# Graph layer with 4 nearest neighbours on one core: x times W2 at the opening of the score stage, scaled rows stored once in fp32

## The chip, the cores and the metric

One core of one Trainium2 chip runs the program. The metric is device time in microseconds (us); lower is better. All matrices are fp32; "fp32r" marks the rounded form that TensorE multiplies in one pass.

## The reference, cut to what matters

```
d  = 1/sqrt(rowsum(A));   y = d * (A @ (d * x))          # A: 8192 x 8192, x: 8192 x 128
z  = leaky_relu(y @ W1 + b1, 0.1)
S  = exp(-sqrt(max(|z_i - z_j|^2, 0) + 1e-10) / 2), all but the 4 largest of each row set to 0
A2 = S + A;  d2 = 1/sqrt(rowsum(A2))
out = d2 * (A2 @ (d2 * x)) @ W2 + b2
result = layernorm(x + out)
```

## The kernel before

Rows are cut into 64 tiles of 128, 16 blocks of 512 (four tiles each) and 8 groups of 1024. Three engines' programs and a DMA queue are written out by hand; every engine works its own list in order, and semaphores tie the lists together.

**First stages (to about 1045 us).** A is read, summed by rows and multiplied with d * x * W1, then read again in part, and z is made, kept as a rounded half `zh` and a rest `zl`.

**Score stage (1045 to 2240 us).** For each tile j of each group g, TensorE makes 8 pairs of 128x512 scores (`scores`, lines 881 to 889), ScalarE copies each pair out of PSUM (line 1171) and from the third tile on writes squares into PSUM ahead of some pairs (`seed`, line 1156), and VectorE searches the 8 largest of the whole row and their places (`find`, lines 1654 and 1657). There are two score buffers: the copies of tile j wait for the search of tile j-2 (line 1163), the search of tile j for all its copies. Between the second and the third tile TensorE rebuilds rows of squares (`squares_row`), and the third tile waits for their copies (`copy_squares`). From the seventh tile on, A @ xg of the previous group is woven in: SyncE loads pieces of A, ScalarE and GpSimd round them (lines 1141, 1323), GpSimd makes the rests (line 1328), TensorE multiplies (lines 925, 926, 936). Once per group GpSimd works out d2 (`near_sums`, `scale_of_rows`), scales the group's rows of x (`scale_xg`), and splits them into a rounded half `xgh` (`high_of_xg`) and a rest `xgl` (`low_of_xg`). SyncE then stores three things (lines 705 to 709): xg as plain rows to `xs_dram` for the gathers, and both halves to `xh_dram` and `xl_dram`; then it loads the next group's x.

**Tail (from about 2240 us).** 124 "quads" of A, 1 MB each, are loaded by SyncE through six slots (`load_t`). 92 are rounded by ScalarE (`round_t`, line 1220), their rests made by VectorE (`rest_t`, line 1701) and multiplied by TensorE with both halves of the scaled rows (`quad`, lines 995 to 1001); 32 are plain fp32 products (line 985). The halves come back from DRAM, two 512 KB loads for each of seven groups (`load_xs`). Each block is finished beside the quads, in the order `FIN` and at the quads `FIN_AT` (f counts blocks in that order): GpSimd gathers 4 neighbour rows for each row with 16 indirect DMAs a block (line 1485), ScalarE weighs them (`weigh`, line 1231), VectorE adds them (`neighbours`), TensorE adds the sum to the block by products with the identity (`gathered`, line 1012); ScalarE or VectorE brings it to SBUF (`heavy_y`, `light_y`), TensorE multiplies by W2 (`times_w2`, line 1021), VectorE adds x and b2 and takes the moments, ScalarE normalizes and stores. The blocks of `LIGHTS` (0 to 8) have most of their sum made in the score stage; they are kept in `acc`.

```
for u in range(len(tail)):
    quad(u)
    for f in range(B):
        if u == FIN_AT[f]:
            gathered(f)
        if u == FIN_AT[f] + 2:
            times_w2(f)
times_w2(B - 1)
```

Of the kernel before, what the change touches and what calls it, by code (L numbers as in the profile page):

```python
# [34 lines left out]
W1_EARLY = 3  # L35
STEP_2 = 3
# [10 lines left out]
FIN_AT = (22, 28, 34, 41, 48, 55, 62, 69, 76, 83, 90, 97, 103, 109, 115, 123)  # L47
OPEN_T, SUM_AFTER, ACC_AT = 6, 4, (9, 20, 40)
# [81 lines left out]
def build(nc, x, xt, at, W1, b1, W2, b2, consts, out, xs_dram, xh_dram, xl_dram, acc_dram, d_dram):  # L130
# [48 lines left out]
    with ctx:  # L179
# [88 lines left out]
        yz_odd = sb("yz_odd", [P, 2, BC], at=top_of["xgl_odd"])  # L268
        y = (tmp[:, 0:BC], yz_odd[:, 0])
# [21 lines left out]
        for name, where in (("raw_sq", top_of["sqn"]), ("raw_z", top_of["zl"] + 3 * SLOT * 4),  # L291
                            ("raw_ring", top_of["ring"] + 3 * SLOT * 4)):
            raw_t.append(sb(name, [P, TB, BC], at=where)[:, :, :])

# [61 lines left out]
        sq_turned = sem("sq_turned")  # L356
        z2_ok = sem("z2_ok")
# [30 lines left out]
        s_split = sem("s_split")  # L388
# [22 lines left out]
        u_ok = sem("u_ok")  # L411
        yf_light = sem("yf_light")
# [119 lines left out]
        n_light = [sum(b in LIGHTS for b in FIN[:f + 1]) for f in range(B)]  # L532
        n_heavy = [f + 1 - n_light[f] for f in range(B)]
# [16 lines left out]

        def wait_yf(eng, f):

            if FIN[f] in LIGHTS:
                eng.wait_ge(yf_light, n_light[f])
            else:
                eng.wait_ge(yf_heavy, n_heavy[f])
# [101 lines left out]
        def _(sp):  # L658
# [30 lines left out]
            sp.dma_start(xg, x[:, 0:GT]).then_inc(s_xn, 16)  # L689

            def group_loads(g, odd, first):
                xgh_g, xgl_g = halves_of(odd)
                for k in range(count(g)):
# [8 lines left out]
                    if k == RAW - 1 + (NP0 // 2 if first else 0):  # L702
# [3 lines left out]
                        dst = xh_dram[bass.ds(g, 1)].rearrange("o p t d -> p (o t) d")  # L706
                        sp.dma_start(dst, xgh_g[:, :, :].bitcast(F32)).then_inc(s_split, 16)
                        dst = xl_dram[bass.ds(g, 1)].rearrange("o p t d -> p (o t) d")
                        sp.dma_start(dst, xgl_g[:, :, :].bitcast(F32)).then_inc(s_split, 16)
                    if k == RAW + (NP0 // 2 if first else 0):  # L710
                        sp.wait_ge(s_xg, 16 * (g + 1))
                        sp.dma_start(xg, x[:, bass.ds((g + 1) * GT, GT)]).then_inc(s_xn, 16)
# [15 lines left out]
            def load_xs(g):  # L728
                low = g if g < G - 2 else G - 1
                sp.dma_start(xsh[:, g * GT:(g + 1) * GT].bitcast(F32), xh_dram[g]).then_inc(s_xs[g], 16)  # L730
                dst = (xsl if g < G - 2 else xsh)[:, low * GT:(low + 1) * GT].bitcast(F32)
                sp.dma_start(dst, xl_dram[g]).then_inc(s_xs[g], 16)

            sp.wait_ge(s_split, 32 * (G - 1))
# [31 lines left out]
        def _(pe):  # L766
# [125 lines left out]

            def squares_row(i):
# [12 lines left out]
            def piece(g, odd, k):  # L906
# [8 lines left out]
                if opens(g, k):  # L915
                    if not (is_first(g) and u < BANKS):
                        pe.wait_ge(flushed, units_before(g) + u - BANKS + 1)
                    if k == 0:
                        pe.wait_ge(xg_ok, chain_of(g, is_first(g)))
# [20 lines left out]
            def group_pe(g, odd):  # L940
                for j in range(GT):
                    for c in range(NE):
# [7 lines left out]
                        if is_first(g) and (j, c) == (0, NE // 2):  # L950
                            turn_squares(1)
                        if is_first(g) and (j, c) == (PLAIN_TILES - 1, NE - 1):
# [16 lines left out]
            def quad(u):  # L969
# [20 lines left out]
                pe.wait_ge(s_xs[h * TB // GT], 32)  # L990
# [14 lines left out]
            def gathered(f):  # L1005
                light = FIN[f] in LIGHTS
                bank = PS[:, 4 + f % 2] if light else PS[:, (FIN[f] - HB) % 2]
                if f >= 2:
                    wait_yf(pe, f - 2)
                pe.wait_ge(gs_ok, TB * (f + 1))  # L1010
                for j in range(TB):
                    i = pe.matmul(bank[:, j * P:(j + 1) * P], gs[f % 2][:, j], ident[:, :],
# [796 lines left out]
```

## Time and profile before

| | before |
|---|---|
| median of 3 runs | 2687.81 us (2685.91 to 2693.51) |
| profiled execution, its own time | 2688.38 us |
| profiled execution, span | 2686.4 us |
| busy share PE / DVE / ACT / POOL | 92 / 86 / 60 / 45% |
| mean granted TensorE clock | 0.982 |

PE is TensorE, DVE VectorE, ACT ScalarE, POOL GpSimd, SP SyncE. A busy TensorE is modelled: a matmul of 512 columns shows 0.39 us but the next starts 0.23 us later. An fp32 product shows as two records, a rounded one as one. Times of rows are counted from the span's start.

### The profile page before, as it was taken

Reading aid. Unit: us, or ns where it says so; the run is one execution under the profiler, and the core shown is the slowest. Engines: PE = TensorE matmul, PEld = TensorE weight load, DVE = VectorE, ACT = ScalarE, POOL = GpSimd, SP = SyncE. Lnnn points to the kernel's source line nnn. Section 1 sums busy time; section 2 is a strip of 40 time slices with the busy share of each in tenths; the row PEclk is TensorE's granted clock in tenths of the full one; section 3 lists DMA queues with packets and bytes.
Section 4 is the critical chain, followed back from the end, with each engine's and each line's share of the span. In section 5 each row is a group of like instructions: output and inputs, shape, how many; then the busy total and the mean of one; then the engine's idle time right before and its main releaser. Section 6 shows DMA issues by size and latency. Waiting matters only on the chain.

```text
span 2686.4 us, 28877 instructions
## 1 busy us (share of the span) xinstructions
PE 2463.0 (92%) x9309; PEld 1707.4 (64%) x9309; DVE 2313.1 (86%) x1366; ACT 1607.0 (60%) x1811; POOL 1198.3 (45%) x987
## 2 busy tenths in 40 slices
PE   0467999999999999899999999999999998899998
PEld 0233444444577776577778787877778775566765
DVE  7998889886788887999999999989999877587886
ACT  0000000000276766899999999989998885477775
POOL 0000000000000000067787878778787895777772
PEclk9879999999999999999999999999999998999999
DMA  9999999997599991035555555546555569999995
GB/s 389 421 394 407 398 421 420 421 403 293 197 413 360 363 349 55 0 114 177 150 167 150 166 152 154 161 133 183 143 175 146 177 181 351 397 401 394 392 379 215
DMA packets 150332, 722.74 MB, mean 269 GB/s; under 512 B 19424, under 2 KB 27296, under 8 KB 88992
## 3 DMA queue, kind: packets, MB, share of 16 engines
q1 hardware_dynamic: 124384, 670.43, 66.5%
q0 software_dynamic: 18800, 37.77, 5.8%
q10 hardware_dynamic: 6992, 12.62, 1.4%
q8 instruction: 79, 1.29, 0.2%
q14 instruction: 77, 0.63, 0.1%
HBM read 684.53 MB, written 36.21 MB: 268 GB/s over the span
## 4 chain that ended last, share of the span: by engine, by line
PE 56%; ACT 13%; issue 10%; DVE 9%; DMA 8%; POOL 3%; SPq 0%; ACTq 0%; POOLq 0%; DVEq 0%
PE PS L779 19%; ACT R L1171 5%; PE PS L881 4%; PE PS L883 4%; PE PS L882 4%; DMA ring<-at 3%; PE PS L985 3%; PE PS L849 3%; PE PS L925 2%; PE PS L936 2%; PE PS L926 2%; DVE R L1654 2%; ACT PS L1156 2%; PE PS L845 2%; PE PS L846 2%
## 5 line engine op out<-in xcount | busy, mean ns | idle before, releaser
L1328 POOL TENSOR_TENSOR al<-ring,ah 128x1024 fp32r<-128x1024 f32 x264 | 643.6, 2439 | 179.7 <-ACT ah L1141 168.1
L1654 DVE MAX8 R<-R 128x8 f32<-128x8192 f32 x64 | 555.8, 8685 | 59.4 <-ACT R L1171 59.2
L1171 ACT ACTIVATE R<-PS 128x1024 f32<-128x1024 f32 x512 | 518.0, 1018 | 116.1 <-PE PS L889 85.9
L1657 DVE FIND_INDEX8 R<-R,R 128x8 uint32<-128x8192 f32 x64 | 555.8, 8685 | 0.0
L1301 POOL CAST zst<-zh 128x128 fp32r<-128x128 f32 (+1 forms) x64 | 26.3, 411 | 1112.7 <-DVE zl L1577 811.6
L881 PE MATMUL PS<-zh,zst 128*128 128x512 f32 x1024 | 407.8, 398 | 29.0 <-ACT PS L1156 12.1
L883 PE MATMUL PS<-zh,zst 128*128 128x512 f32 x1024 | 400.3, 391 | 0.0
L882 PE MATMUL PS<-zl,zst 128*128 128x512 f32 x1024 | 399.7, 390 | 0.0
L1485 POOL DMA_INDIRECT R<-xs_dram,R x256 | 283.8, 1109 | 86.1 <-issue 77.1
L1156 ACT ACTIVATE PS<-R 128x1024 f32<-128x1024 f32 x310 | 318.0, 1026 | 6.6
L779 PE MATMUL PS<-cache,R 128*128 128x512 f32 x584 | 259.6, 596 | 5.4 <-DVE R L1528 5.4
L1510 DVE TENSOR_TENSOR R<-R,cache 128x2048 f32<-128x2048 f32 x106 | 242.9, 2292 | 17.5 <-DMA cache<-at 15.0
L881 PEld LDWEIGHTS PS<-zh,zst 128*128 128x128 f32 x1024 | 192.4, 188 | 96.3 <-ACT PS L1156 24.9
L883 PEld LDWEIGHTS PS<-zh,zst 128*128 128x128 f32 x1024 | 192.5, 188 | 41.6
L882 PEld LDWEIGHTS PS<-zl,zst 128*128 128x128 f32 x1024 | 192.7, 188 | 38.9 <-issue 0.7
L779 PEld LDWEIGHTS PS<-cache,R 128*128 128x128 f32 x584 | 110.7, 191 | 140.2 <-issue 140.2
L779 PE MATMUL PS<-ring,R 128*128 128x512 f32 x384 | 176.4, 606 | 9.9 <-DVE R L1528 5.4
L1585 DVE TENSOR_TENSOR al<-ring,ah 128x2048 fp32r<-128x2048 f32 x66 | 151.0, 2290 | 30.7 <-ACT ah L1053 30.2
L1510 DVE TENSOR_TENSOR R<-R,ring 128x2048 f32<-128x2048 f32 x72 | 165.0, 2291 | 12.3 <-DMA ring<-at 10.4
L995 PE MATMUL PS<-ah_t,xsh 128*128 128x512 f32 x368 | 155.4, 422 | 18.6 <-ACT ah_t L1220 18.4
L1060 ACT ACTIVATE R<-PS 128x512 f32<-128x512 f32 x16 | 9.6, 597 | 255.8 <-PE PS L788 255.8
L1141 ACT ACTIVATE ah<-ring 128x1024 fp32r<-128x1024 f32 x152 | 159.7, 1051 | 3.3 <-DMA ring<-at 2.6
(190 smaller groups left out, 4376.4 us busy)
## 6 DMA issues: line engine op xcount, KB each, us to landing
R<-at SPq DMA_DIRECT2D x152, 1024.0 KB, 11.0
ring<-at SPq DMA_DIRECT2D x148, 1024.0 KB, 9.6
ring<-at SPq DMA_DIRECT2D x264, 512.0 KB, 3.9
cache<-at SPq DMA_DIRECT2D x117, 1024.0 KB, 17.1
raw_sq<-at SPq DMA_DIRECT2D x21, 1024.0 KB, 9.8
raw_z<-at SPq DMA_DIRECT2D x20, 1024.0 KB, 10.1
raw_ring<-at SPq DMA_DIRECT2D x20, 1024.0 KB, 8.6
acc_dram<-R POOLq DMA_DIRECT2D x78, 256.0 KB, 5.7
```

The costliest lines, as they stand in the source:

```text
L779: i = pe.matmul(PS[:, b % YB], xs[:, q * TB + k], slots_a[slot_of[n]][:, k], start=first and k == 0, stop=prod_at[b, q] == closed[b] and k ...
L881: pe.matmul(bank, zst[:, par, 0], zh[:, cols], start=not on_seed, stop=False, skip_group_check=True)
L882: pe.matmul(bank, zst[:, par, 0], zl[:, cols], start=False, stop=False, skip_group_check=True)
L883: i = pe.matmul(bank, zst[:, par, 1], zh[:, cols], start=False, stop=on_seed, skip_group_check=True)
L1141: act.activation(ah[:, k % SPLIT], raw[k % RAW], ACT.Copy).then_inc(rounded, 1)
L1156: act.activation(pair(False, 0, c), sq_row[c], ACT.Copy).then_inc(seeded, 1)
L1171: act.activation(score[j % 2][:, c * EC:(c + 1) * EC].rearrange("p (b c) -> p b c", b=2), pair(first, j, c), ACT.Copy).then_inc(copied, 1)
L1328: pool.tensor_tensor(al[:, k % SPLIT], raw[k % RAW], ah[:, k % SPLIT].bitcast(F32), ALU.subtract)\
L1485: pool.indirect_dma_start(gx[f % 2][:, j, m], None, xs_dram, bass.IndirectOffsetOnAxis(ap=sidx[:, FIN[f] * TB + j, m:m + 1], axis=0))\
L1510: v.tensor_tensor(total.rearrange("p (k c) -> p k c", c=BC), other, slots_a[slot_of[n]], ALU.add)\
L1654: v.max(top[:, j], score[j % 2]).then_inc(dve3, 1)
L1657: v.max_index(place[:, j], top[:, j], score[j % 2]).then_inc(placed, 1)
```

## The change

x is multiplied by W2 before anything else is done with it in the second half, so that A2 @ (d2 * x) comes out already multiplied. Eight products of eight tiles each are put into the first group's second to fifth tile; their result goes through PSUM banks 4 and 5 and `xw_out` to `xw_dram`, from which the groups are loaded in place of x. In the tail the product with W2 becomes a transposition; the gathered rows, now multiplied by W2 too and weighed by S * d2, are added by VectorE to x and b2, so `gathered` and `light_y` go. Of the scaled rows one more fp32 copy is stored (`xp_dram`) in place of two halves; in the tail it is loaded once per group, ScalarE rounds it (`high_of_xs`) and GpSimd subtracts (`low_of_xs`). The waits on `s_split` go; SyncE waits for `s_xp` ahead of the next group's load.

```diff
+W2_AT = [(j, c) for j in range(1, 5) for c in (2, 6)]
+LOW_AFTER = {4: (0, 0), 5: (0, 3), 6: (1, 2)}
# SyncE, ahead of the first group
-            sp.dma_start(xg, x[:, 0:GT]).then_inc(s_xn, 16)
+            sp.wait_ge(zl_ok, B)
+            for k in range(G):
+                if k >= 1:
+                    sp.wait_ge(w2_made, k)
+                sp.dma_start(xt_in[:, :, :], xt[:, k * GT:(k + 1) * GT]).then_inc(s_xt, 16)
+                if k >= 1:
+                    sp.wait_ge(w2_copied, k)
+                    sp.dma_start(xw_dram[:, (k - 1) * GT:k * GT], xw_out[:, :, :]).then_inc(s_xw, 16)
+                if k == 2:
+                    sp.wait_ge(s_xw, 16)
+                    sp.dma_start(xg, xw_dram[:, 0:GT]).then_inc(s_xn, 16)
...
# SyncE, each group
-                        sp.dma_start(dst, xgh_g[:, :, :].bitcast(F32)).then_inc(s_split, 16)
-                        dst = xl_dram[bass.ds(g, 1)].rearrange("o p t d -> p (o t) d")
-                        sp.dma_start(dst, xgl_g[:, :, :].bitcast(F32)).then_inc(s_split, 16)
+                        sp.dma_start(dst, xg).then_inc(s_xp, 16)
...
+                        sp.wait_ge(s_xp, 16 * (g + 1))
# SyncE, tail
-                sp.dma_start(xsh[:, g * GT:(g + 1) * GT].bitcast(F32), xh_dram[g]).then_inc(s_xs[g], 16)
...
-                sp.dma_start(dst, xl_dram[g]).then_inc(s_xs[g], 16)
+                sp.dma_start(low_tiles(g).bitcast(F32), xp_dram[g]).then_inc(s_xs[g], 16)
# TensorE
+            def x_w2(k):
+                pe.wait_ge(s_xt, 16 * (k + 1))
...
+                    pe.wait_ge(w2_copied, k)
+                for j in range(GT):
+                    i = pe.matmul(PS[:, 4 + j // TB, j % TB * P:(j % TB + 1) * P], xt_in[:, j], w2[:, :],
+                                  start=True, stop=True)
+                i.then_inc(w2_made, 1)
...
-                pe.wait_ge(s_xs[h * TB // GT], 32)
+                pe.wait_ge(xs_low, h * TB // GT + 1)
...
-                    i = pe.matmul(PS[:, 6 + f % 2, j * P:(j + 1) * P], yf[f % 2][:, j * P:(j + 1) * P], w2[:, :],
-                                  start=True, stop=True)
+                    i = pe.transpose(PS[:, 6 + f % 2, j * P:(j + 1) * P], rows[:, j * P:(j + 1) * P], ident[:, :])
...
-                    if u == FIN_AT[f]:
-                        gathered(f)
# ScalarE
+            def copy_x_w2(k):
+                act.wait_ge(w2_made, k + 1)
+                if k >= 1:
+                    act.wait_ge(s_xw, 16 * k)
+                act.activation(xw_out[:, :, :].rearrange("p (h j) d -> p h (j d)", h=2), PS[:, 4:6], ACT.Copy)\
+                   .then_inc(w2_copied, 1)
...
+                        if first and (j, c - 1) in W2_AT:
+                            copy_x_w2(W2_AT.index((j, c - 1)))
...
+            def high_of_xs(g):
+                act.wait_ge(s_xs[g], 16)
+                act.activation(xsh[:, g * GT:(g + 1) * GT], low_tiles(g).bitcast(F32), ACT.Copy).then_inc(xs_high, 1)
...
+                    if u == tail.index((HB, g * GT // TB)) - 1:
+                        high_of_xs(g)
# GpSimd
-                pool.tensor_copy(sval[:, tiles], near[:, lo:hi])
+                pool.tensor_tensor(sval[:, tiles_of(g, early_part)], near[:, lo:hi], bcast(tiny[:, 4, lo:hi], KNN),
+                                   ALU.mult).then_inc(sval_ok, 1)
...
+            def low_of_xs(g):
+                pool.wait_ge(xs_high, g + 1)
+                pool.tensor_tensor(low_tiles(g), low_tiles(g).bitcast(F32), xsh[:, g * GT:(g + 1) * GT].bitcast(F32),
+                                   ALU.subtract).then_inc(xs_low, 1)
# low_of_xs(0 to 3) stand ahead of the gathers, the other three after gathers (f, j) of LOW_AFTER
# VectorE
-            def light_y(f):
...
+                v.wait_ge(gs_ok, TB * (f + 1))
+                lt(v.tensor_tensor(xb[f % 2], xb[f % 2], gs[f % 2], ALU.add))
```

## Rows read from the trace of the kernel before

**Rows 1.** The page: the span.

```profile
span 2686.4 us, 28877 instructions
```

**Rows 2.** Stretches: length; busy us of PE, PEld, DVE, ACT, POOL; clock, DMA share, GB/s.

```profile
1045.00:1190.00 145.00, 124.75 (x502) 92.38 (x501) 137.97 (x26) 122.62 (x130) 36.49 (x49) 0.99 0.11 35
2240.00:2330.00 90.00, 75.83 (x233) 46.33 (x234) 52.59 (x54) 37.35 (x48) 53.13 (x45) 0.91 1.02 401
2330.00:2640.00 310.00, 299.74 (x1250) 215.04 (x1248) 254.43 (x480) 222.83 (x357) 241.36 (x216) 1.00 1.01 391
```

**Rows 3.** Timeline of VectorE, opening: start us, us, instruction, [idle before it].

```profile
1065.12 8.68 DVE L1654 MAX8 R<-R 128x8 f32<-128x8192 f32 x1
...
1086.07 8.70 DVE L1654 MAX8 R<-R 128x8 f32<-128x8192 f32 x1 [3.36 <-ACT R L1171]
```

**Rows 4.** Timeline of ScalarE, opening of the score stage.

```profile
1060.83 1.02 ACT L1171 ACTIVATE R<-PS 128x1024 f32<-128x1024 f32 x1 [0.78 <-PE PS L889]
...
1084.00 1.92 ACT L1171 ACTIVATE R<-PS 128x1024 f32<-128x1024 f32 x2
...
1103.71 1.03 ACT L1171 ACTIVATE R<-PS 128x1024 f32<-128x1024 f32 x1 [2.44 <-DVE R L1657]
```

**Rows 5.** Groups by line, whole run: busy us, mean ns | idle before, releasers.

```profile
L1328 POOL TENSOR_TENSOR al<-ring,ah 128x1024 fp32r<-128x1024 f32 x264 | 643.6, 2439 | 179.7 <-ACT ah L1141 168.1 <-PE PS L936 1.2 <-POOL d2s L1383 1.0
L1485 POOL DMA_INDIRECT R<-xs_dram,R x256 | 283.8, 1109 | 86.1 <-issue 77.1 <-DMA xs_dram<-R 8.4 <-DVE R L1715 0.6
L1141 ACT ACTIVATE ah<-ring 128x1024 fp32r<-128x1024 f32 x152 | 159.7, 1051 | 3.3 <-DMA ring<-at 2.6 <-PE PS L926 0.5
...
L1012 PE MATMUL PS<-ident,R 128*128 128x128 f32 x128 | 16.8, 274 | 0.0
...
L1727 DVE TENSOR_TENSOR R<-R,b2r 128x512 f32<-128x512 f32 x16 | 10.9, 682 | 0.0
...
L1722 DVE TENSOR_TENSOR R<-PS,R 128x512 f32<-128x512 f32 x9 | 6.2, 688 | 8.7 <-PE PS L1012 8.6
...
L814 PE MATMUL PS<-ident,dsc 128*64 128x128 f32 x1 | 0.3, 273 | 0.0
```

**Rows 6.** Waits, 2330 to 2640 us: us in total, times, longest.

```profile
ACT ah_t L1220 <- PE PS L1001: 30.1, 20, 4.6
...
ACT ah_t L1220 <- DMA raw_z<-at: 9.2, 3, 3.4
```

**Rows 7.** DMA issues, whole run: KB each, median us from issue to landing.

```profile
R<-xs_dram,R POOLq DMA_INDIRECT x256, 5.9
...
xs_dram<-R SPq DMA_DIRECT2D x7, 512.0 KB, 3.5
xsh<-xh_dram SPq DMA_DIRECT2D x7, 512.0 KB, 14.3
```

**Rows 8.** Timeline of GpSimd, gathers of the tail.

```profile
2275.32 1.06 POOL L1485 DMA_INDIRECT R<-xs_dram,R  x1 [8.36 <-DMA xs_dram<-R]
...
2611.77 0.94 POOL L1485 DMA_INDIRECT R<-xs_dram,R  x1 [0.30 <-issue]
...
2627.46 1.97 POOL L1485 DMA_INDIRECT R<-xs_dram,R  x1 [0.30 <-issue]
...
2635.72 1.14 POOL L1485 DMA_INDIRECT R<-xs_dram,R  x1 [0.30 <-issue]
```

**Rows 9.** Timeline of VectorE, at 2627 us.

```profile
2627.40 2.35 DVE L1701 TENSOR_TENSOR al_t<-raw_sq,ah_t 128x1024 fp32r<-128x1024 f32 x2
```

**Rows 10.** Timeline of ScalarE: last weighing of the last two blocks.

```profile
2628.77 0.40 ACT L1231 ACTIVATE R<-R,sval_t 128x128 f32<-128x128 f32 x1 [0.43 <-ACT R L1249]
...
2657.50 0.68 ACT L1231 ACTIVATE R<-R,sval_t 128x128 f32<-128x128 f32 x2
```

**Rows 11.** Chain that ended last, end of the tail: start us, us.

```profile
2676.06 0.91 PE PS L1012 x8
...
2677.64 1.17 PE PS L1021 x8
```

More of the change, by code:

```diff
@@ L127, in plan_tail, with build @@
     return quads
-def build(nc, x, xt, at, W1, b1, W2, b2, consts, out, xs_dram, xh_dram, xl_dram, acc_dram, d_dram):
+def build(nc, x, xt, at, W1, b1, W2, b2, consts, out, xs_dram, xp_dram, acc_dram, d_dram, xw_dram):
     loads, products, two = plan_ab()
@@ L293, in build, with low_tiles @@
             raw_t.append(sb(name, [P, TB, BC], at=where)[:, :, :])
+        def low_tiles(g):
+            low = g if g < G - 2 else G - 1
+            return (xsl if g < G - 2 else xsh)[:, low * GT:(low + 1) * GT]
         def low_tile(t):
@@ L356, in build @@
         sq_turned = sem("sq_turned")
+        sq_read = sem("sq_read")
+        sval_ok = sem("sval_ok")
+        s_xt = sem("s_xt")
+        w2_made = sem("w2_made")
+        w2_copied = sem("w2_copied")
+        s_xw = sem("s_xw")
         z2_ok = sem("z2_ok")
@@ L387, in build @@
         flushed = sem("flushed")
-        s_split = sem("s_split")
+        s_xp = sem("s_xp")
+        xs_high = sem("xs_high")
+        xs_low = sem("xs_low")
         s_xs = [sem(f"s_xs{k}") for k in range(G - 1)]
@@ L530, in is_first @@
             return isinstance(n, int) and n == 0
-        n_light = [sum(b in LIGHTS for b in FIN[:f + 1]) for f in range(B)]
-        n_heavy = [f + 1 - n_light[f] for f in range(B)]
+        n_heavy = [sum(b in HEAVIES for b in FIN[:f + 1]) for f in range(B)]
         plain = [h >= LAST for b, h in tail]
@@ L951, in group_pe @@
                             turn_squares(1)
+                        if is_first(g) and (j, c) in W2_AT:
+                            x_w2(W2_AT.index((j, c)))
                         if is_first(g) and (j, c) == (PLAIN_TILES - 1, NE - 1):
@@ L1003, in quad, with turn_y @@
                 i.then_inc(prod_t, 1)
[L1005 to L1012, printed above, removed]
-                                  start=light, stop=True, skip_group_check=True)
-                i.then_inc(u_ok, 1)
-            def times_w2(f):
-                wait_yf(pe, f)
+            def turn_y(f):
+                b = FIN[f]
+                if b in LIGHTS:
+                    pe.wait_ge(light_ok, b + 1)
+                    rows = acc[:, b * BC:(b + 1) * BC]
+                else:
+                    pe.wait_ge(yf_heavy, n_heavy[f])
+                    rows = yf[f % 2]
                 if f >= 2:
@@ L1234, in heavy_y @@
             def heavy_y(f):
-                act.wait_ge(u_ok, f + 1)
+                act.wait_ge(prod_t, tail.index((FIN[f], B - 1)) + 1)
                 if f >= 2:
@@ L1265, in _ @@
                     round_t(u)
+                for g in range(1, G - 1):
+                    if u == tail.index((HB, g * GT // TB)) - 1:
+                        high_of_xs(g)
                 for i, b in enumerate(ROWS_X):
@@ L1400, in high_of_xg @@
                     pool.wait_ge(prodb, pieces_before(g - 1))
-                    hold(pool)
-                    pool.wait_ge(s_split, 32 * (g - 1))
                     hold(pool)
@@ L1488, in _ @@
                             .then_inc(s_gx[f % 2][j], 16)
+                    for g, after in LOW_AFTER.items():
+                        if (f, j) == after:
+                            low_of_xs(g)
         @block.vector
@@ L1673, in last_near_sums @@
                 v.wait_ge(r2_ok, chain_of(g, False))
-                lk(v.tensor_copy(sval[:, g * GT:T], near))
             def last_scale_of_rows(lk):
@@ L1679, in last_scale_of_rows @@
                 lk(v.tensor_copy(d2s[:, (G - 1) * GT:T], tiny[:, 4]))
+                v.tensor_tensor(sval[:, (G - 1) * GT:T], near, bcast(tiny[:, 4], KNN), ALU.mult).then_inc(sval_ok, 1)
             def scale_last_xg(g):
@@ L1767, in _ @@
                         neighbours(f, u - FIN_AT[f] + 6)
-                    if u == FIN_AT[f] + 1 and FIN[f] in LIGHTS:
-                        light_y(f)
                     if u == FIN_AT[f] + 2:
```

55 lines of the change are left out of this document (28 added, 27 removed).

## The prediction, made before the change was built

> **What bounds the kernel now.** I read the span first [rows 1] and then the stretches the change touches [rows 2], because each has its own limit. The opening of the score stage, 1045 to 1190 us, is VectorE's: 138 of 145 us busy, with the DMA engines at a share of 0.11. There the timelines of VectorE and ScalarE [rows 3, 4] tell who waits for whom: VectorE starts its second search at 1065.12, 3.3 us after the last copy it needs (1060.83 + 1.02 = 1061.85), and idles 3.36 us before the third, at 1086.07, whose copies end at 1085.92. From the fifth tile on ScalarE waits for VectorE (2.44 us at 1103.71), so VectorE sets the pace from there.
>
> In the tail the DMA engines are full from 2240 to 2640 us, share 1.01 to 1.02 at 391 to 401 GB/s, and from 2330 TensorE is busy for 299.7 of 310 us as well [rows 2]. The waits say which is first: ScalarE stood 30.1 us for TensorE to give rounded halves back and 9.2 us for a load into one slot [rows 6]. TensorE leads, the DMA engines are at its heels. A third stream runs beside them: 256 gathers issued from 2275.32 to 2636.86 us without any wait but issue [rows 5, 8], 361.5 us or 1.41 us each. Its room is what ScalarE leaves it. The last gather of block 14 in finishing order starts at 2611.77 and lands about 5.9 us later [rows 7], at 2617.7; ScalarE weighs it at 2628.77 [rows 10], 11.1 us on. For the last block it is 2641.6 against 2657.50, 15.9 us.
>
> **The change part by part.**
>
> Opening. Four fp32 products of a tile, eight records, take 0.91 us [rows 11], so one of the new products of eight tiles takes 1.82, and its copy out of PSUM 1.03, as the like copies of scores [rows 4]. Two products stand in the second tile: 3.64 us. Its copies then end at 1065.5, and the second search starts 0.4 late. But the rebuilt rows of squares and the third tile follow in order, so they start 3.64 later. In the third tile ScalarE's alternating copies and seeds set the pace; one of its two new copies stands ahead of the last score copy, 1.03, and I add 0.3 for the part of a product that TensorE's gaps don't take. VectorE already waits for this tile, so its third search comes 3.64 + 1.03 + 0.3 = **5.0 us** later. In the fourth and fifth tiles the two copies (2.06) fit into the 2.44 us for which ScalarE waits. The bounds are 0 (all in gaps) and 8 x (1.82 + 1.03) = 22.8; I stay near the low end, as only the second and third tiles lack room. Every later tile waits for the search two tiles before, so the 5.0 us is carried to the end.
>
> At nothing there: the 8.4 MB of loads and stores (DMA share 0.11 [rows 2]; a 512 KB transfer lands in 3.5 us [rows 7], and a product comes four pairs of scores after the one that frees its buffer; behind its wait stand that tile's scores, so a late load would cost its lateness). On SyncE the loads of the first three pieces and of the first x move behind the eighth product; they are needed in the seventh tile, over a tile later.
>
> Groups. SyncE issues one 512 KB store less and waits for another one's landing ahead of the next x load; the piece loads are queued behind that wait. A store's landing (3.5 us) in seven groups would be 24.5 at worst; at best the loads' whole share of ScalarE's rounding waits, 2.6 us, goes [rows 5]. With only 2.6 us of waiting for loads in the stage there is depth to hide the wait, so 0. The multiplied `sval` replaces a copy on GpSimd: 0. The dropped `s_split` wait was for stores long landed: 0.
>
> Tail, work. TensorE loses 16 x 0.91 = 14.6 us of identity products; a transposition has one record where a product has two (lines 814 and 1012 [rows 5]), so 16 x 0.45 = 7.3 more, together 21.9 (14.6 if a transposition takes as long as a product). VectorE loses nine additions of 0.69 and the 8.7 us they waited, and gains 16 of 0.68 [rows 5]: 4.0 less. ScalarE gains 7 x 1.05 = 7.4 and GpSimd 7 x 2.44 = 17.1 [rows 5], four of GpSimd's seven ahead of its gathers, where it waits anyway (8.36 us for its store [rows 8]). The loads lose seven times 512 KB [rows 7], 3.67 MB or 9.2 us at 401 GB/s.
>
> Tail, what comes of it. TensorE's 21.9 can't come out while the DMA engines are full; their 9.2 can. And the gathers come later: three subtractions stand among them, 3 x 2.44 = 7.3. Each such subtraction waits for ScalarE's rounding, which waits for a load; queued behind are the next gathers, and behind those ScalarE's weighing and rounding. The load stands ahead of its quad's own in SyncE's queue, so I add no wait.
>
> VectorE's new additions hold gathers up as well. A gather takes 0.94 us undisturbed; the one at 2627.46 took 1.97 [rows 8] beside VectorE's two subtractions at 2627.40 [rows 9]. All 256 take 283.8 - 256 x 0.94 = 43 us more than undisturbed, beside some 296 us of VectorE work (254 of 310 [rows 2], times 361), 0.15 us per us. So 10.9 us more of additions make 1.6. The Trainium skill speaks the other way here: SBUF — State Buffer, Who interferes with whom, has it (as an inference) that a two-input VectorE operation takes the read side of the port it shares with GpSimd, while making DMA descriptors needs the write side. By that the term would be 0 and the sum 1.6 lower. The rows on the gathers disagree, and I go by them.
>
> So the gathers are 8.9 us later. Of the room 2.2 us is left at block 14 and 7.0 at the last. The tail can be at most 2.2 us ahead at block 14; in the 28.7 us between the two weighings TensorE has 1.8 less to do (one identity product, two transpositions) and six filled slots to draw on, so I take 5.5 ahead at the last (between 4.0 and 7.0). Behind it one identity product (0.91) and some 0.7 of the last W2 product (1.17 [rows 11]) leave the chain: 1.6. Tail: **7.1 us** less.
>
> Sum: 5.0 - 7.1 = -2.1 us. The profiled execution's own time is 2688.4 (span and 2.0 around it), 0.6 above the median of the runs; from the median I predict 2687.8 - 2.1 = **2685.7 us**. A measurement of this kernel tells about 0.3%, 8.1 us, from no change.
>
> **The rivals.**
>
> *The gathers don't bind, TensorE's relief comes out* (0.29). For it: TensorE is the one waited for [rows 6], and rooms of 11 to 16 us may suffice if VectorE disturbs gathers less than before. Against: DMA share 1.01. In full, 5.0 - 21.9 = -16.9, 2671; with the DMA engines' 9.2 and the end's 1.6 and half of the rest, 2677.
>
> *The gathers bind hard* (0.13), the case on the slow side. Each of the three subtractions on GpSimd can wait for VectorE's pair of subtractions (2.35 [rows 9]): 7 more; and all 10.9 us of additions may hold gathers: 9 more. The stream is then up to 25 us late against a room of 11.1. From about 18 late the tail gains nothing; at 22 it loses 4, and with the opening it makes 2687.8 + 9 = 2697. For it: no slack inside the stream; against: most gathers run undisturbed (mean 1.11 against 0.94).
>
> *It doesn't do what it says: the fewer bytes free nothing*, because six slots, not bytes, hold the loads back. Then only the end's 1.6 remains: 2687.8 + 5.0 - 1.6 = 2691, within 0.3% like the forecast; I count it there (0.58 together).
>
> **How the numbers follow.** The likeliest case is no change that can be told: 2685.7, own range 2680 to 2692. Chances: faster by over 0.3% 0.29, within 0.58, slower 0.13. For eight in ten the range takes in most of the first rival and the start of the second: 2672 to 2696.
>
> **What would show it.** Right: VectorE idle some 8 us before the third search and none before the fourth; the last gather issued some 34 us before the span's end, where it was 49.5 (2686.4 - 2636.9), with ScalarE waiting for a gather at its weighing of block 14 or nearly so; TensorE's busy share in the steady tail down to some 90% with the DMA share still 1.0. Wrong: third search on its old time (opening hidden) or over 10 us late; no wait at any weighing and a tail shorter by over 12 us (first rival); waits for gathers from the first blocks on (second). A search of the fourth or fifth tile that also comes late would break the opening's sum.

## The result, and the profile after

The changed kernel takes 2695.94 us (median of 20 runs, 2689.18 to 2700.16), the kernel before 2688.36 beside it (20 runs): ratio 1.0025, 95% interval 1.0019 to 1.0031, so 5 to 8 us slower. The forecast was 2685.7 us. The profiled execution took 2697.97 us, with a span 9.4 us longer than before [rows 1].

The page's span and busy times:

```profile
span 2695.8 us, 28724 instructions
...
PE 2463.5 (91%) x9245; PEld 1702.8 (63%) x9245; DVE 2326.3 (86%) x1373; ACT 1621.4 (60%) x1826; POOL 1224.2 (45%) x994
```

The same stretches as [rows 2], and 20 us early in the tail (length; busy us of PE, PEld, DVE, ACT, POOL; clock, DMA share, GB/s):

```profile
1045.00:1190.00 145.00, 133.55 (x609) 104.35 (x608) 132.67 (x26) 125.04 (x132) 32.13 (x46) 0.98 0.29 98
2240.00:2330.00 90.00, 69.74 (x217) 42.99 (x215) 58.57 (x53) 46.78 (x55) 62.51 (x40) 0.92 0.99 383
2320.00:2340.00 20.00, 12.47 (x33) 7.18 (x33) 9.60 (x12) 8.71 (x18) 16.18 (x15) 0.83 0.80 306
2330.00:2640.00 310.00, 288.47 (x1068) 195.19 (x1068) 250.25 (x471) 214.88 (x352) 244.64 (x216) 0.98 0.99 382
```

TensorE is busy for 93% of the steady tail in place of 97%, and the DMA engines are nearly as full as before, but in 2320 to 2340 their share is 0.80. In the opening VectorE has lost some 5 us of 138. VectorE's timeline there shows where, beside [rows 3]:

```profile
1066.04 8.70 DVE L1707 MAX8 R<-R 128x8 f32<-128x8192 f32 x1 [0.47 <-ACT R L1201]
...
1091.47 8.70 DVE L1707 MAX8 R<-R 128x8 f32<-128x8192 f32 x1 [7.82 <-ACT R L1201]
...
1108.99 8.67 DVE L1707 MAX8 R<-R 128x8 f32<-128x8192 f32 x1
```

It idles 7.82 us before the third search, where it idled 3.36, and not at all before the fourth. The waits of 2330 to 2640 us, beside [rows 6]:

```profile
ACT ah_t L1252 <- PE PS L1032: 38.8, 21, 7.7
...
ACT R L1265 <- DMA R<-xs_dram,R: 13.2, 5, 4.5
...
PE PS L1026 <- POOL xsh L1512: 7.5, 1, 7.5
```

Two waits are new. ScalarE waits for gathers at five weighings, and TensorE stands 7.5 us for GpSimd's subtraction of group 6. (At the tail's start, outside this window, TensorE also stands 5.8 us for the subtraction of group 0, where before it stood 3.5 us for ScalarE's rounding.) GpSimd's timeline shows that subtraction, queued among the gathers, and the last gather, beside [rows 8]:

```profile
2283.25 1.91 POOL L1535 DMA_INDIRECT R<-xs_dram,R  x1 [3.52 <-DMA xs_dram<-R]
...
2289.39 2.37 POOL L1512 TENSOR_TENSOR xsl<-xsl,xsh 128x1024 fp32r<-128x1024 f32 x1
...
2309.09 2.35 POOL L1512 TENSOR_TENSOR xsl<-xsl,xsh 128x1024 fp32r<-128x1024 f32 x1
...
2329.09 2.49 POOL L1512 TENSOR_TENSOR xsh<-xsh 128x1024 fp32r<-128x1024 f32 x1
...
2658.38 0.99 POOL L1535 DMA_INDIRECT R<-xs_dram,R  x1 [0.30 <-issue]
```

The last gather ends at 2659.37, 22.5 us later than before. ScalarE waits once early, 4.2 us at the second block finished. Then it waits for gathers under 0.5 us until block 14 in finishing order (counted from 0, the last but one), and there it waits at all four tiles. The longest of these waits, in its timeline:

```profile
2625.29 1.28 ACT L1265 ACTIVATE R<-R,sval_t 128x128 f32<-128x128 f32 x4 [4.55 <-DMA R<-xs_dram,R]
```

Groups by line, beside [rows 5] (busy us, mean ns | idle before, releasers):

```profile
L1535 POOL DMA_INDIRECT R<-xs_dram,R x256 | 291.6, 1139 | 80.8 <-issue 75.4 <-DMA xs_dram<-R 3.5 <-DVE R L1766 1.8
...
L1772 DVE TENSOR_TENSOR R<-R 128x512 f32<-128x512 f32 x16 | 11.2, 697 | 0.6
L1047 PE MATMUL PS<-ident,R 128*128 128x128 f32 x64 | 9.7, 275 | 0.7 <-ACT R L1272 0.7
```

**Where the 9.4 us are.** The searches show it, each against its time before. The first comes 0.4 late, the third to eighth 5.4, the last 7.2; the span ends 9.4 late. So the opening costs 5.0, the rest of the score stage 1.8, and the tail 2.1, where 7.1 less were forecast. One profile tells a tail's length only to some 3 us: the tail of the kernel before was itself 2.2 us longer in the profile of the first experiment below, which leaves it as it is, and the changed kernel's was 2.7 shorter in that of the second. So it is shown that the tail gained nothing like 7.1, but not that it lost 2.1. The theory: the three subtractions and slower gathers put the gathers so late that they set the end. Its rivals: the transfers or TensorE set it, or TensorE's wait for group 6 alone does.

### The profile page after: what moved, and what is told of

The parts are those of the page before. It is cut to its first block, busy times and chain, and to the rows that moved or that the text cites. A ratio compares the mean times of both kernels' runs of the same rounds, so it can differ in the third digit from the quotient of the medians.

```text
span 2695.8 us, 28724 instructions
## 1 busy us (share of the span) xinstructions
PE 2463.5 (91%) x9245; PEld 1702.8 (63%) x9245; DVE 2326.3 (86%) x1373; ACT 1621.4 (60%) x1826; POOL 1224.2 (45%) x994
## 4 chain that ended last, share of the span: by engine, by line
PE 51%; issue 12%; ACT 12%; DVE 11%; DMA 7%; POOL 6%; SPq 0%; POOLq 0%; ACTq 0%; DVEq 0%
PE PS L795 18%; DMA ring<-at 5%; PE PS L897 4%; PE PS L899 4%; PE PS L898 4%; ACT R L1201 4%; PE PS L954 2%; PE PS L955 2%; PE PS L965 2%; PE PS L865 2%; DVE al_t L1754 2%; DVE R L1707 2%; POOL R L1535 2%; ACT ah_t L1252 2%; PE PS L1016 2%
## 5 line engine op out<-in xcount | busy, mean ns | idle before, releaser
L1535 POOL DMA_INDIRECT R<-xs_dram,R x256 | 291.6, 1139 | 80.8 <-issue 75.4
```

The source lines that it names most:

```text
L1535: pool.indirect_dma_start(gx[f % 2][:, j, m], None, xs_dram, bass.IndirectOffsetOnAxis(ap=sidx[:, FIN[f] * TB + j, m:m + 1], axis=0))\
```

## The experiments

Each ran beside the kernel before on one chip, in five rounds where no other number is given. "Tail" below is the profiled execution's span less the time of its last search, against the kernel before. In the four sets of runs the kernel before took 2688.4 to 2690.3 us, so medians of different sets compare less well than their ratios to it.

### The opening alone

The kernel before with the opening's loads, products, copies and stores, whose results nothing uses.

```diff
 # kernel before
+                        if is_first(g) and (j, c) in W2_AT:
+                            x_w2(W2_AT.index((j, c)))
...
+                        if first and (j, c - 1) in W2_AT:
+                            copy_x_w2(W2_AT.index((j, c - 1)))
```

> The kernel before, with the opening products alone: eight loads, products, copies and stores in the second to fifth tile, whose results nothing uses. Theory A (the opening's 5.0 us are carried to the end): third search 5.0 us later, none before the fourth, 2692.5 to 2694.5, ratio 1.0015 to 1.0025. Theory B (the score stage or the tail makes the time good): within 2 us of the kernel before. If the shift also grows by some 1.8 us from the eighth to the last search, as in the changed kernel, the product of weights and d2 and the fp32 store have no part in that.

Measured: 2695.09 us, ratio 1.0019 (1.0010 to 1.0028), so 2.7 to 7.5 us slower. VectorE's timeline:

```profile
1065.92 8.69 DVE L1696 MAX8 R<-R 128x8 f32<-128x8192 f32 x1 [0.46 <-ACT R L1211]
...
1091.37 8.69 DVE L1696 MAX8 R<-R 128x8 f32<-128x8192 f32 x1 [7.84 <-ACT R L1211]
```

Theory A holds: the ratio is in its range, and the time 0.6 us above it because the kernel before took 2690.32 us beside it. The third search comes 5.05 us later against the first, and the loss is carried to the end. From the eighth search to the last the shift grows by 0.6 only, so most of the changed kernel's 1.8 comes from something else in the change.

### Opening products one tile later

```diff
-W2_AT = [(j, c) for j in range(1, 5) for c in (2, 6)]
+W2_AT = [(j, c) for j in range(2, 6) for c in (2, 6)]
```

> The eight opening products stand one tile later (third to sixth tile). Theory A (only the second and third tile lack room: 3.64 us of products ahead of the rebuilt rows, 1.33 for one copy and the rest of a product in the third tile): VectorE's idle time before the third search falls from 7.8 us to some 4.2, every later search comes 3.7 us earlier than in the changed kernel, and the time falls by 3.0 to 4.0 us. Theory B (a product and its copy cost TensorE and ScalarE wherever they stand): the searches of the fourth to seventh tile get idle time of their own, some 2 us each, and the time stays within 1 us of the changed kernel.

Measured: 2690.27 us, ratio 1.0008 (0.9998 to 1.0017). The third search is 2.6 us late against the first, the sixth 0.8 more: 3.4 in place of 5.0. The median is 5.7 below the changed kernel's, more than these 1.6 explain; the profile's tail is 2.7 shorter, within its scatter. So neither theory in full: the second tile's 3.67 are gone, but the third tile now loses 2.6 and not 1.3. Part of that is the clock: at the start of the third tile TensorE ran at half its clock for longer. The windows of this kernel, from the tile's first product:

```profile
1065.00:1069.00 4.00, 3.85 (x9) 3.12 (x10) 4.00 (x1) 1.08 (x3) 0.00 (x0) 0.50 0.01 4
1069.00:1071.00 2.00, 2.00 (x6) 1.52 (x6) 1.85 (x3) 1.97 (x2) 0.00 (x0) 0.50 0.00 0
```

and of the changed kernel, whose first product there starts at 1072.48:

```profile
1072.00:1075.00 3.00, 2.52 (x6) 2.07 (x7) 2.85 (x3) 2.35 (x3) 0.00 (x0) 0.56 0.00 0
1075.00:1077.00 2.00, 2.00 (x8) 1.59 (x8) 2.00 (x1) 0.83 (x1) 0.00 (x0) 0.81 0.92 301
```

### Three products a tile, and the product of weights and d2 off the chain

```diff
+W2_AT = [(j, c) for j in (3, 4, 5) for c in (0, 3, 6)][:8]
...
+                pool.sem_inc(d2_ok, 1)
                 pool.tensor_tensor(sval[:, tiles_of(g, early_part)], near[:, lo:hi], bcast(tiny[:, 4, lo:hi], KNN),
                                    ALU.mult).then_inc(sval_ok, 1)
...
-                pool.sem_inc(d2_ok, 1)
```

> The eight opening products stand in the fourth to sixth tile (three, three, two), and GpSimd's product of weights and d2 follows the signal that releases the scaling, instead of standing ahead of it. Theory A (the opening costs only where a tile's chain has no room; the 1.8 us over the groups are that product on the chain, some 0.25 us a group): no idle time is added before the third search, at most 1.5 us before the fifth to seventh, and from the eighth to the last search the shift grows by under 0.6 us instead of 1.8. Theory B (three products a tile overfill TensorE, and the groups' share is SyncE's wait for the fp32 store): 3 us or more before the fifth to seventh search, and the shift over the groups grows by 1.5 us or more as before.

Measured (one run): 2696.83 us. Theory B on the opening: the fourth search is 1.0 late, the fifth 2.9, the sixth 7.0, more than with the products where the change has them. The growth over the groups was 3.9 us, so moving the product of weights and d2 didn't remove it.

### Earlier subtractions among the gathers

```diff
-LOW_AFTER = {4: (0, 0), 5: (0, 3), 6: (1, 2)}
+LOW_AFTER = {4: (0, 0), 5: (0, 2), 6: (1, 0)}
```

> The subtractions of groups 5 and 6 on GpSimd stand 4 and 8 gathers... earlier among the gathers (after the third tile of the first block and after the first tile of the second). Theory A (the tail's saved 9.2 us of transfers were lost when TensorE stood 7.5 us for the subtraction of group 6, queued behind gathers, and the loads ran dry: DMA share 0.80 at 2320 to 2340): that wait falls under 1 us, the share in that stretch rises over 0.95, the rounding at the middle of the tail comes 3 to 5 us earlier, and the time falls by 0 to 4 us, because the gathers, which end at the same time as in the changed kernel, then stop ScalarE for longer at the last blocks. Theory B (the transfers' rate sets the middle of the tail whatever TensorE waits): middle and end unchanged within 1 us.

Measured: 2697.0 us, ratio 1.0031 (1.0020 to 1.0042): no gain. TensorE's wait for group 6 is gone and the DMA share at 2320 to 2340 is 1.02, but the rounding at the middle of the tail (the 46th of 92) came 0.7 us later and not 3 to 5 earlier, and ScalarE's waits for gathers from 2240 to 2695 us doubled, from 15.0 to:

```profile
ACT R L1265 <- DMA R<-xs_dram,R: 30.2, 14, 5.7
```

One wait took the other's place. So TensorE's wait by itself was not what held the tail.

### No addition of the neighbour sums

```diff
-                v.wait_ge(gs_ok, TB * (f + 1))
-                lt(v.tensor_tensor(xb[f % 2], xb[f % 2], gs[f % 2], ALU.add))
```

> VectorE's 16 additions of the weighed neighbour sums to x and b2 are left out, so the output lacks the neighbours; the gathers, weighings and pairwise additions remain. Theory A (these additions, both inputs in SBUF, hold GpSimd's gathers back, and the gathers bind the last two blocks): the mean of a gather falls from 1.139 us to 1.12 or less, the last one ends 4 to 8 us earlier against the first, ScalarE's waits for gathers fall from 13 us to 5 to 9, and the time falls by 2 to 6 us. Theory B (the gathers' lateness comes from the three subtractions and the waits alone): mean and end of the gathers unchanged within 1 us, time within 1.5 us of the changed kernel.

Measured: 2695.07 us, ratio 1.0020 (1.0011 to 1.0029). The gathers did get faster, as theory A has it:

```profile
L1535 POOL DMA_INDIRECT R<-xs_dram,R x256 | 286.1, 1118 | 80.0 <-issue 77.1 <-DMA xs_dram<-R 2.8
```

The gathers take 5.5 us less without 11.2 us of additions. But ScalarE's waits for gathers didn't fall (15.4 us from 2240 to 2695, against 15.0 in the changed kernel), the median fell by 0.9 only and the intervals overlap, so the time didn't settle it; TensorE still waited 4.7 us for group 6. The profile, with a tail 6.0 us shorter than the changed kernel's, is of the fastest of the 11 runs, 4.2 us below their median.

### Both at once

```diff
-LOW_AFTER = {4: (0, 0), 5: (0, 3), 6: (1, 2)}
+LOW_AFTER = {4: (0, 0), 5: (0, 2), 6: (1, 0)}
...
-                lt(v.tensor_tensor(xb[f % 2], xb[f % 2], gs[f % 2], ALU.add))
```

> The subtractions of groups 5 and 6 stand earlier among the gathers, and VectorE's 16 additions of the neighbour sums are left out (the output lacks the neighbours). Each alone brought back under 2 us. Theory A (two limits side by side: TensorE's wait for group 6, which lets the loads run dry, and late gathers; lifting one leaves the other): together they bring back 4 to 7 us, to within 3.5 us of the kernel before. Theory B (neither is what holds the tail): 2694 to 2697 as before.

Measured: 2692.16 us, ratio 1.0014 (1.0004 to 1.0023), 3.8 us below the changed kernel's median and 3.2 above the kernel before: just under theory A's lower end, and the intervals still overlap.

### The subtractions of groups 4 to 6 on VectorE

```diff
-LOW_AFTER = {4: (0, 0), 5: (0, 3), 6: (1, 2)}
+LOW_AFTER = {}
...
                     rest_t(u)
+                for g in range(4, G - 1):
+                    if u == tail.index((HB, g * GT // TB)) - 1:
+                        v.wait_ge(xs_high, g + 1)
+                        v.tensor_tensor(low_tiles(g), low_tiles(g).bitcast(F32),
+                                        xsh[:, g * GT:(g + 1) * GT].bitcast(F32), ALU.subtract).then_inc(xs_low2, 1)
```

> The three subtractions among the gathers (groups 4 to 6) move from GpSimd to VectorE, behind its rest of the quad ahead of the one that needs them. Theory A (subtractions queued among gathers cost twice: the gathers come 7.5 us later, and TensorE waits for the halves): TensorE's wait for group 6 falls from 7.5 to under 2 us, the gathers take 367 to 370 us from first to last instead of 376, ScalarE's waits for gathers fall under 8 us, and the time falls by 3 to 7 us against the changed kernel, which brings it to within 4 us of the kernel before. Theory B (VectorE, at some 83% busy, becomes the one waited for, and its own subtractions hold the gathers): the time stays within 1.5 us of the changed kernel.

Measured: 2690.2 us, ratio 0.9997 (0.9988 to 1.0006): 5.7 us below the changed kernel: theory A by the time. ScalarE's waits for gathers, though, did not fall under 8 us: they are 15.9, against 15.0 in the changed kernel. With the opening still 5.0 us late, the tail is now shorter than before (1.8 us in the profiled execution). TensorE no longer waits for group 6, and the stretch that ran dry is full:

```profile
2320.00:2340.00 20.00, 20.00 (x63) 11.57 (x62) 9.24 (x14) 10.42 (x19) 15.39 (x16) 1.00 1.02 398
```

The gathers take 370.3 us from first to last, not 376.1. The 46th of 92 roundings comes 5.1 us earlier against the last search than before the change; in the changed kernel it comes 1.5 later.

### The same, with the gathers held up again

```diff
 # on top of the version above, on GpSimd
+                    if (f, j) in ((0, 0), (0, 3), (1, 2)):
+                        for m in range(4):
...
+                            pool.tensor_tensor(zst[:, 0, :, :], zst[:, 1, :, :], zst[:, 1, :, :].bitcast(F32),
+                                               ALU.subtract).then_inc(delay, 1)
```

> Subtractions of groups 4 to 6 on VectorE, and twelve small subtractions on unused data put among the gathers on GpSimd at the places where they stood: the gathers come late again, TensorE's halves don't. Theory A (late gathers alone suffice to hold the tail): the last gather ends 7 to 10 us later than with VectorE's subtractions alone, ScalarE waits 25 us or more for gathers, and the time rises by 4 to 7 us against that version (2690.2). Theory B (the halves' lateness was the whole cost): within 1.5 us of it.

Measured: 2702.64 us, ratio 1.0051 (1.0038 to 1.0063). The gathers take 382.8 us, 12.5 more than without the delay. Against the last search, the last gather of block 14 starts 9.5 us later, its weighing comes 8.0 later and the span ends 8.1 later. So late gathers alone hold the tail, nearly one for one. The medians, from two sets, are 12.4 apart, where 4 to 7 were expected. ScalarE's waits:

```profile
ACT R L1272 <- DMA R<-xs_dram,R: 32.7, 16, 4.7
```

### The kernel before, with its gathers held up

The same twelve subtractions, in the kernel before.

> The kernel before, with twelve small subtractions on unused data put among GpSimd's gathers at the three places where the changed kernel has its three (some 7 to 9 us in all). Theory A (the room of 11.1 us at block 14 and 15.9 us at the last is real): the last gather ends 7 to 9 us later, ScalarE waits under 1 us for gathers, and the time stays within 1.5 us of the kernel before. Theory B (a gather held up costs the tail directly): 4 to 9 us slower.

Measured: 2688.8 us, ratio 0.9995 (0.9986 to 1.0004). The gathers took 374.7 us, 13.2 more than before: 8.4 are the twelve subtractions, and 4.5 are longer gathers (288.3 us in all, before 283.8), with no addition added. The median shows no cost. But ScalarE waited 7.0 us for gathers, where under 1 was expected, all of it at the second and third block finished, and the tail of the profile is 3.9 us longer. So the kernel before had room for about that much and hardly more.

### Both halves stored and loaded as before

```diff
-                        dst = xp_dram[bass.ds(g, 1)].rearrange("o p t d -> p (o t) d")
-                        sp.dma_start(dst, xg).then_inc(s_xp, 16)
+                        sp.dma_start(dst, xgh_g[:, :, :].bitcast(F32)).then_inc(s_split, 16)
...
+                        sp.dma_start(dst, xgl_g[:, :, :].bitcast(F32)).then_inc(s_split, 16)
...
```

> Both halves are stored and loaded as before the change, W2 stays first: GpSimd's seven subtractions and ScalarE's seven roundings in the tail go, 3.67 MB of loads come back, SyncE's wait for the fp32 store goes. Theory A (the tail lost its gain to subtractions queued among gathers and to late gathers): TensorE's waits for them are gone, the gathers end some 7 us earlier against the first, ScalarE waits under 3 us for gathers, and the tail is 3 to 9 us shorter than in the changed kernel although 9.2 us of transfers are back. Theory B (the transfers' bytes set the tail): the tail is 5 to 9 us longer than in the changed kernel. The groups' share (1.8 us over seven groups) stays if the product of weights and d2 on GpSimd causes it, and goes if SyncE's wait does.

Measured: 2688.87 us, ratio 0.9998 (0.9989 to 1.0007): 7 us below the changed kernel, theory A. ScalarE waits for no gather; it waits for loads. The tail is 5.4 us shorter than before, all of it in its second half: against the last search the 46th rounding is 0.5 us late, the 92nd and last 4.0 early. All 256 gathers take 286.2 us, with the additions in place. The growth over the groups is 2.8 us although SyncE's wait for the fp32 store is gone.

### Combinations

Stored halves and the opening and product of the three-a-tile run:

> Both halves stored and loaded as before the change, opening products in the fourth to sixth tile, the product of weights and d2 behind the signal. If the opening's 5 us and the groups' 2 us add to the tail's gain of some 5 us as separate terms: 2681 to 2684 us, ratio to before 0.9975 to 0.9985. If a term comes back elsewhere (the tail starts earlier but the transfers set its end): no better than 2687.

Measured: 2690.23 us, ratio 0.9999 (0.9990 to 1.0008). The second case. The tail is 4.9 us shorter than before, but the opening costs 6.9 here, so the terms to be added were wrong.

VectorE's subtractions with the same opening:

> fp32 rows stored once, subtractions of groups 4 to 6 on VectorE, opening products in the fourth to sixth tile, the product behind the signal. If the saved 9.2 us of transfers come out once nothing queues behind the gathers: below the version with stored halves, 2676 to 2682. If the gathers bind the last blocks or the first halves come late: 2683 to 2689, no better than the version with stored halves, with ScalarE waiting 5 us or more for gathers.

Measured: 2692.59 us, ratio 1.0011 (1.0002 to 1.0021); ScalarE waited 13.6 us for gathers: the second case, and slower still than its 2683 to 2689.

VectorE's subtractions, and the last group's rows earlier:

```diff
                     s_of_distances(G - 1)
+                    root_of_sums(G - 1)
                 if u == BY_POOL + 1:
-                    root_of_sums(G - 1)
...
                     last_near_sums(lk)
-                if u == BY_POOL + 2:
                     last_scale_of_rows(lk)
...
```

> Beside the subtractions of groups 4 to 6 on VectorE, the last group's rows are scaled and stored earlier: ScalarE's last square root stands right behind its exponential, VectorE's scaling ahead of its rest of the fourth quad, GpSimd's store ahead of its subtraction of group 2. Theory A (the gathers bind the last blocks): the first gather comes some 4 us earlier against the last search than with VectorE's subtractions alone, the last gather too, and the time falls by 2 to 4 us against that version (2690.2). Theory B (the end is set by TensorE or the transfers): the earlier gathers become room, the time stays within 1.5 us of it.

Measured: 2689.61 us, ratio 1.0001 (0.9992 to 1.0010). The first gather came 3.4 us earlier against the last search, the last 2.1; the time can't be told from the version without it, as theory B has it.

With the opening one tile later as well:

> The version before this one with the opening products one tile later (third to sixth tile), which cost 3.4 us of searching there in place of 5.0. If the terms add: 1.6 us faster than the version before this one, ratio to the kernel before 0.998 to 0.9995. If they don't: equal to it.

Measured: 2686.8 us, ratio 0.9983 (0.9965 to 1.0001): 2.8 us below the version without it, where the terms to be added made 1.6, but not told from the kernel before.

That version, with the weighings and VectorE's additions of the neighbours two quads later:

```diff
-                    if 0 <= u - FIN_AT[f] + 7 < TB:
-                        weigh(f, u - FIN_AT[f] + 7)
+                    if 0 <= u - FIN_AT[f] + 5 < TB:
+                        weigh(f, u - FIN_AT[f] + 5)
...
```

> The fastest version so far (subtractions of groups 4 to 6 on VectorE, last rows early, opening products one tile later), with ScalarE's weighings and VectorE's neighbour additions two quads later, which gives the gathers some 5 us more room. Theory A (late gathers hold its last blocks): ScalarE's waits for gathers fall from 13.6 to under 3 us and the time falls by 3 to 5 us to 2681 to 2684. Theory B (the end is set elsewhere): within 1.5 us of 2686.8.

Measured: 2683.89 us, ratio 0.9982 (0.9973 to 0.9990): faster than both kernels, by 2.7 to 7.3 us than the one before. The gathers still bind: ScalarE waited 23.6 us for them, not under 3. That the tail ran ahead until it met them would explain it, but isn't shown.

```profile
2652.57 1.95 POOL L1540 DMA_INDIRECT R<-xs_dram,R  x1 [0.30 <-issue]
```

From the end of that last gather to the span's end (2682.8) it is 28.3 us; in the changed kernel it is 36.4.

The changed kernel with the earlier subtractions and later weighings:

> The changed kernel with the subtractions of groups 5 and 6 earlier among the gathers, and the weighings and neighbour additions two quads later: TensorE's wait for group 6 goes, and the gathers, as late as they are, get some 5 us more room; everything is computed. Theory A (two limits side by side): ScalarE's waits for gathers fall from 30 us to under 12, and the time falls by 3 to 6 us against the changed kernel, to 2690 to 2693. Theory B: 2695 to 2698, as with the earlier subtractions alone.

Measured: 2690.8 us, ratio 1.0012 (1.0002 to 1.0022). The time came out as theory A has it, 5.1 us below the changed kernel's median. The waits didn't: 51.6 us, at 21 weighings.

## Why the prediction was wrong

**Opening, +5.0: right, the last 1.37 with some luck.** Against the first search, the second tile's copies end 3.67 us later (3.64 forecast), the third search 5.03 later; the third tile's own part is 1.37 (1.33 forecast). That no later search would wait was right, and the opening alone bore it out. But other executions of the same opening put the third search 3.5 to 6.3 us later (last section), so an agreement to 0.1 us is luck.

**Groups, 0: 1.8 too low.** The shift grows from 5.4 to 7.2 between the eighth and the last search. It is no scatter: it grows by 1.6 to 4.1 in every version of the changed kernel, and by -0.1 and 0.6 in the two that keep the groups of the kernel before. Neither SyncE's wait nor the product on GpSimd's chain is shown to cause it: without the wait it was 2.8, with the product behind its signal 1.7 to 3.9. In five of the runs (stored halves, two with three products a tile, the last rows earlier, and VectorE's subtractions with delayed gathers) 1.5 to 1.8 us of it came in one step, at the 41st tile; in the changed kernel 0.9 came at the 60th. The cause stays open.

**Tail, -7.1: it was +2.1.** TensorE's work came out as costed (a transposition is one record of 0.275 us, where a product was two [rows 5]). What failed is the lateness of the gathers. The place where they bind was foreseen, block 14 in finishing order, with a room of 11.1 us. Its last gather in GpSimd's timeline, and its last weighing in ScalarE's, beside [rows 8, 10]:

```profile
2635.55 1.17 POOL L1535 DMA_INDIRECT R<-xs_dram,R  x1 [0.30 <-issue]
...
2641.52 0.40 ACT L1265 ACTIVATE R<-R,sval_t 128x128 f32<-128x128 f32 x1 [1.32 <-DMA R<-xs_dram,R]
```

The gather starts 23.8 us later than before, 16.5 net of the score stage, where 8.9 were forecast. 16.5 against a room of 11.1 leaves the weighing 5.4 late; it came 5.5 late, where the forecast had it 2.2 early. The 78th of the 92 roundings, some 26 us earlier, was only 0.3 late, so this came at block 14. The rule holds in other profiles: 13.8 late made 2.8 with the opening one tile later, 20.5 made 9.6 with VectorE's subtractions and delayed gathers. From there to the span's end are 54.3 us, before 57.7: 3.4 less, where the forecast had 3.3 + 1.6 = 4.9. And 5.5 - 3.4 is the 2.1 by which the tail grew. That last stretch hardly varies: it was 54.2 to 54.3 us in all 13 versions of the changed kernel that leave the weighings where they are, and none of them waited for a gather of the last block. So what a late gather costs is decided at block 14.

The 16.5 us are made of four parts. The first gather gave 0.7 (0 forecast); the three subtractions 2.37 + 2.35 + 2.49 = 7.2 (7.3); the gathers themselves, up to this one, 9.0 (1.6); the gaps between them took back 0.4. So the step that failed is the term "10.9 us more of additions make 1.6", the only one that let gathers grow longer: a mean over all of VectorE's work, 0.15 us per us. Over all 256 gathers, 291.6 - 283.8 = 7.8 us stand in its place.

How much of this the additions made is only in part shown. Leaving them out took 5.5 us off the gathers, and 5.0 with the earlier subtractions (286.1 us both times). But with stored halves and all additions the gathers took 286.2 and 287.8 us, only 2.4 and 4.0 more than before, and the delay alone made them 4.5 us longer in the kernel before. And 1.8 of the 7.8 us are there even with nothing to hold a gather up: the shortest gather takes 0.940 us in the kernel before and in every version that stores halves, and 0.947 or more in every version that stores the fp32 copy. Over 256 gathers 0.007 us make 1.8. Why is open, and with it how the 7.8 us divide.

"So I add no wait", for the subtractions, was wrong as well: I named the gathers behind the waiting instruction, but not TensorE, which waits for its result; it stood 7.5 us. Taking this wait away alone gained nothing, as the earlier subtractions showed.

The Trainium skill (SBUF — State Buffer, Who interferes with whom) would have put the additions' hold on gathers at 0, as an inference. The trace disagrees more than I had allowed: 286.1 us of gathers without them, 291.6 with them.

**The rivals.** The second, that the gathers bind hard (0.13), came nearest, 2695.9 where it gave 2697, but in part by luck: the subtractions took 2.4 us each, where it had them wait 7 us more for VectorE; at 16.5 late its own rule still left the tail a gain; and 1.8 us came from the groups. The first would have needed the gathers out of the way. The third, that the saved bytes free nothing, is against the middle of the tail with VectorE's subtractions, 5.1 us ahead, where stored halves were 0.5 behind.

**What would show it.** Four signs came as named: 7.8 us idle before the third search and none before the fourth; the last gather issued 37 us before the end (34 forecast); ScalarE waiting at block 14; TensorE 93% busy with a share of 0.99. They fit both the forecast and its slow rival, so they could not tell the two apart. A sign of the rival, waits for gathers from the first blocks on, came in part: 4.2 us at the second block, then under 0.5 until block 13 was done. What would have told them apart is the time of block 14's last weighing against the last search: 2.2 us earlier by the forecast, 5.5 later in the trace.

## What to carry to other kernels

Work put into a queue is paid at the queue's place and at everything that waits for its result: a subtraction set between gathers delayed the gathers and starved TensorE, and moving it within the queue only swapped the two. Before a stream without slack is lengthened, work out from the trace how long each of its items lies ready before it is used. The least of these is the room, and it need not be at the last item: here it was 11.1 us at the last block but one, and that figure held. The lateness to set against it is harder: a mean hold (all extra time over all overlap) doesn't price one kind of instruction, and a stream that is moved lies beside other work than before.

## What the hardware did that was not expected

**What holds a gather up.** A least-squares fit of the 256 gathers of the kernel before against what VectorE did beside each gives nearly 0.4 us of hold per us of the rests (both inputs in SBUF), 0.5 to 0.6 for the addition of b2, and 0.1 to 0.2 for the additions and the multiply-add that read PSUM; the changed kernel's fit gives nearly 0.4 for the rests again and -0.1 to 0.1 for those that read PSUM. Single small groups scatter in it. For the added additions it gives only 0.1, but 0.8 for those of b2, which run right ahead of them; the two taken as one give 0.5. The removed additions read PSUM, the added ones don't, so by the fit nine for sixteen was no fair exchange. No run tried the two kinds alone. By the fit a part of the growth is more company: the rests lay beside the gathers for 150 us in place of 144, as the later gathers did in the kernel before (149 us).

**The third tile's clock.** TensorE idles some 2 us between the rebuilt rows of squares and the third tile, and the tile then starts at a granted clock of 0.5, its lower level of 1.2 GHz. The kernel before does so as well (0.50 from 1070 to 1072 us). How long that lasts differs between executions of the same opening: 3 us in the changed kernel, 6 us with VectorE's subtractions and delayed gathers, where the idle time before the third search was 9.1 us in place of 7.8:

```profile
1088.02 8.69 DVE L1718 MAX8 R<-R 128x8 f32<-128x8192 f32 x1 [9.12 <-ACT R L1208]
```

So the opening's 5.0 us were between 3.5 and 6.3 in other executions with the same opening, a scatter of the size of some terms that were argued about.
